# Cross attention of a decoder layer on one core: units spread one to a head, offsets and keys in halves, two transposed buffers, positions in 12 operations, clips ahead of unit copies

## The reference

```python
K = k @ Wk.T + bk; V = v @ Wv.T + bv; Qp = q @ Wq.T + bq
off = (Qp @ Woff.T + boff)                  # 16 heads x 5 samples
loc_x = mod(ref + off + loc, sign_lens)
ix = ((loc_x / (key_len - 1) * 2 - 1 + 1) * key_len - 1) / 2
x0 = floor(ix); dx = ix - x0; i0 = x0; i1 = i0 + 1
sk = 0.5 * ((1 - dx) * gather0(Kh, i0) + dx * gather0(Kh, i1))
sv = 0.5 * ((1 - dx) * gather0(Vh, i0) + dx * gather0(Vh, i1))
attn = softmax(einsum(Qh / sqrt(16), sk)); ctx = einsum(attn, sv)
x = layernorm(x + ctx @ Wo.T + bo)
```

## Time and profile before

| | us |
|---|---|
| median of 3 runs | 2228.5 (2226.14 to 2231.98) |
| the profiled execution, its own time | 2223.39 |
| its span in the profile | 2221.6 |
| VectorE's first product of cross attention starts at | 1444.7 |
| VectorE's last product of cross attention starts at | 2021.7 |

### The profile page before, as it was taken

The page is one execution under the profiler, slowest core; times in us unless marked ns, Lnnn a source line. Parts: engine busy times, 40 slices in busy tenths (PEclk is TensorE's granted clock), DMA queues, the critical chain, the costliest instruction groups (busy, mean ns, idle before and its releaser), DMA issues. The chain is left out here.

```text
span 2221.6 us, 42277 instructions
## 1 busy us (share of the span) xinstructions
PE 1860.2 (84%) x16907; PEld 1111.1 (50%) x16907; DVE 1673.1 (75%) x2216; ACT 1311.9 (59%) x1718; POOL 1416.4 (64%) x1067
## 2 busy tenths in 40 slices
PE   5989999999999999999999996487887787883575
PEld 2535545545545545545545543365665565663332
DVE  4876876887887887887797761669769768778676
ACT  2556566656565566566565561286856756873476
POOL 2577877876966976976876873334654554555347
PEclk8989999999999999999999998799988898997796
DMA  6122212202213203213203200100000000100002
GB/s 198 43 48 67 63 44 68 71 16 68 71 35 75 65 15 77 64 33 77 63 16 77 51 23 25 55 3 7 2 7 2 2 2 2 44 2 1 2 1 76
DMA packets 57507, 92.33 MB, mean 42 GB/s; under 512 B 25312, under 2 KB 35552, under 8 KB 53344
## 3 DMA queue, kind: packets, MB, share of 16 engines
q1 hardware_dynamic: 48096, 89.36, 15.6%
q10 hardware_dynamic: 9216, 0.27, 0.2%
HBM read 51.33 MB, written 4.46 MB: 25 GB/s over the span
## 5 line engine op out<-in xcount | busy, mean ns | idle before, releaser
L930 POOL TENSOR_TENSOR acc<-acc,probs 128x1024 f32<-128x1024 f32 (+3 forms) x320 | 593.8, 1856 | 54.3 <-ACT probs L643 24.8
L587 ACT ACTIVATE chunks<-psum 128x1024 bf16<-128x1024 f32 x288 | 281.9, 1026 | 157.6 <-PE psum L453 116.8
L643 ACT ACTIVATE probs<-psum 128x1024 f32<-128x1024 f32 (+3 forms) x384 | 290.7, 812 | 114.8 <-PE psum L494 114.8
L486 PE MATMUL psum<-operands 64*128 64x512 f32 (+3 forms) x1536 | 310.2, 512 | 24.8 <-ACT chunks L587 18.1
L1488 ACT ACTIVATE onehot<-psum 128x1024 bf16<-128x1024 f32 x320 | 323.0, 1038 | 1.3 <-PE psum L1298 1.3
L1895 POOL TENSOR_TENSOR vs<-vs,wgt 128x1280 f32<-128x1280 f32 x64 | 156.3, 2442 | 245.1 <-DVE wgt L1739 245.1
L1316 PE MATMUL psum<-pieces,onehot 128*128 128x64 bf16 x7680 | 289.0, 199 | 25.3 <-ACT vs L1495 18.7
L1316 PEld LDWEIGHTS psum<-pieces,onehot 128*128 128x128 bf16 x7680 | 260.6, 102 | 88.6 <-issue 46.0
L510 PE MATMUL psum<-probs,vals 128*64 128x512 f32 (+3 forms) x1536 | 292.2, 501 | 13.4 <-POOL probs L909 8.3
L786 DVE TENSOR_REDUCE lows<-chunks 128x2 f32<-128x1024 bf16 (+1 forms) x224 | 266.6, 1214 | 22.1 <-ACT chunks L587 12.2
L909 POOL TENSOR_SCALAR_AFFINE_SELECT probs<-probs 128x256 f32<-128x256 f32 x256 | 153.9, 619 | 103.0 <-ACT probs L643 103.0
(11 more groups left out here) (228 smaller groups left out, 3431.4 us busy)
## 6 DMA issues: line engine op xcount, KB each, us to landing
operands<-turned SPq DMA_DIRECT2D x124, 256.0 KB, 5.1
rden<-inverse_rows SPq DMA_DIRECT2D x64, 256.0 KB, 3.9
raw<-in_wqk SPq DMA_DIRECT2D x30, 256.0 KB, 4.4
y<-in_x SPq DMA_DIRECT2D x1, 4096.0 KB, 16.4
wo<-in_wo SPq DMA_DIRECT2D x16, 256.0 KB, 2.7
out<-res SPq DMA_DIRECT2D x16, 256.0 KB, 2.1
raw<-in_wv SPq DMA_DIRECT2D x15, 256.0 KB, 4.3
raw<-in_xT SPq DMA_DIRECT2D x12, 256.0 KB, 3.7
```

What stands on the lines that cost most here:

```text
L486: nc.tensor.matmul(dst[:, hh, 0:width], ops[n % OBUF][rows, 1, kt * P:(kt + 1) * P].bitcast(F32), ops[n % OBUF][rows, 0, a:a + width].bitc ...
L587: nc.scalar.activation(chunks[k % MBUF][:, :, :], slot("max", n, c)[:, :, :], ACT.Copy, scale=-1.0)\
L643: nc.scalar.activation(probs[u % PBUF][:, :, 0:width], slot("s", n, u)[:, :, 0:width], ACT.Exp, scale=1.0 / D ** 0.5).then_inc(s_exp, 1)
L930: G.tensor_tensor(dst, dst, src, ALU.add).then_inc(s_acc, 1)
```

## The change

It changes the following, all in cross attention; everything else is as it was.

- At most one unit stands in a head, at its step 0 (`i0` stays at head 14, step 3): inputs' transposes at heads 0 and 1, offsets in two halves at 2 and 3, `cT` at 4 and 5, keys and values in two halves at 6 and 7, `out` at 8 and 9, queries at 10 and 11.
- `tT` becomes two buffers, `x1T` and `outT`, so that the input's transposes of the next batch can stand while the output's of the batch before are made; the waits on `s_wo` and `s_qd` change with it.
- `locate` has 12 parts with one instruction each, at heads 4, 5, 8, 9, 12 and 13. A table of positions (`ref + loc + folded bias`) is made once and added when the offsets are read.
- ScalarE issues the clips of a step ahead of the unit's copy, for every unit.
- The last batch's input is normalised in the first batch (heads 0 and 3), no longer in the third; statistics of the batch before move to heads 10 and 11, its normalisation to heads 13 and 14, `lengths` to head 3.
- GpSimd's queue follows: `bias_x1` ahead of round 0, `split_kv` ahead of round 1, then `x2_deviations`, `bias_q`, round 2.

```diff
-EARLIER_AT = {(4, 0): ("cT", 0), (4, 2): ("cT", 1), (5, 0): ("out", 0), (5, 2): ("out", 1)}
+EARLIER_AT = {(4, 0): ("cT", 0), (5, 0): ("cT", 1), (8, 0): ("out", 0), (9, 0): ("out", 1)}
-LATER_AT = {(6, 0): ("x1T", 0), (6, 2): ("x1T", 1), (7, 1): ("kv", 0), (8, 1): ("off", 0),
...
+LATER_AT = {(0, 0): ("x1T", 0), (1, 0): ("x1T", 1), (2, 0): ("off", 0), (3, 0): ("off", 1), (6, 0): ("kv", 0),
+            (7, 0): ("kv", 1), (10, 0): ("q", 0), (11, 0): ("q", 1), (14, 3): ("i0", 0)}
-LOCATE_AT = [(9, 2), (9, 3), (10, 1), (10, 3), (11, 1), (11, 3), (12, 1), (12, 3), (13, 1), (13, 3)]
+LOCATE_AT = [(4, 1), (4, 3), (5, 0), (5, 1), (5, 3), (8, 1), (8, 3), (9, 1), (9, 3), (12, 1), (12, 3), (13, 1)]
+X1_STATISTICS_AT = [(0, 1), (0, 2)]
+X1_NORMALISE_AT = [(3, 0), (3, 1), (3, 2), (3, 3)]
+X2_STATISTICS_AT = [(10, 1), (11, 1)]
+X2_NORMALISE_AT = [(13, 2), (13, 3), (14, 0), (14, 1)]
...
-        tT = sb("tT", [P, KT, S])
+        x1T, outT = (sb(name, [P, KT, S]) for name in ("x1T", "outT"))
+        table = sb("positions", [P, TT, HK])
...
                 for u in range(UNITS):
                     use = unit_at(b, h, u)
-                    if use and use[0] == "i0" and n + 1 < HEADS_ALL:
+                    if n + 1 < HEADS_ALL:
                         for k in AHEAD[u]:
                             make_onehot(n + 1, k)
+                    if use:
                         copy_unit(*use)
-                    else:
-                        if use:
-                            copy_unit(*use)
-                        if n + 1 < HEADS_ALL:
-                            for k in AHEAD[u]:
-                                make_onehot(n + 1, k)
                     copy_values(n, u)
...
+            def set_table():
+                st.then(V.tensor_tensor(table[:, :, :], over(ref.unsqueeze(1), [P, TT, HK]),
+                                        over(loc.unsqueeze(2), [P, TT, HK]), ALU.add))
+                dve.wait_ge(s_fold, 1)
+                V.tensor_tensor(bfold[:, :], slot("fold", 0, 0)[:, 1, 0:HK], boff, ALU.add).then_inc(s_foldb, 1)
+                dve.wait_ge(s_foldb, 1)
+                V.tensor_tensor(table[:, :, :], table[:, :, :], over(bfold[:, :].unsqueeze(1), [P, TT, HK]), ALU.add)\
+                 .then_inc(s_table, 1)
...
-                    st.then(V.tensor_scalar(c, a, inv, MAGIC, ALU.mult, ALU.add))
+                    st.done(V.tensor_scalar(c, a, inv, MAGIC, ALU.mult, ALU.add))
+                elif part == 1:
                     st.done(V.tensor_scalar(d, c, MAGIC, size, ALU.subtract, ALU.mult))
...
+                elif part == 7:
+                    dve.wait_ge(s_i0t, b)
+                    st.done(V.tensor_scalar(row, in_pairs(d), MAGIC, None, ALU.subtract))
                 elif part == 8:
-                    dve.wait_ge(s_i0t, b)
-                    for n, src in enumerate((e, d)):
-                        st.done(V.tensor_copy(i0b[:, :, :, HP * NK * n:HP * NK * (n + 1)],
-                                              src.rearrange("p t (g n) -> p t g n", g=NHP)))
+                    st.done(V.scalar_tensor_tensor(out=in_pairs(a), in0=in_pairs(c), scalar=-0.5, in1=row,
+                                                   op0=ALU.add, op1=ALU.subtract))
```

More of the change, by code:

```diff
@@ L1329, in transpose_x1, with project_kv @@
                 last.then_inc(s_x1T, 1)
-            def project_kv(b):
+            def project_kv(b, v):
                 pe.wait_ge(s_in, 32 * (b + 1))
[L1333 to L1338, removed]
+                wait_slot("kv", b, v)
+                dst = slot("kv", b, v)
+                for kt in range(KT):
+                    last = nc.tensor.matmul(dst[:, 0, :], ctxT[:, v, kt, :], wkv[:, kt, :],
+                                            start=kt == 0, stop=kt == KT - 1)
                 last.then_inc(s_kv, 1)
@@ L1643, in read_off @@
-            def read_off(b):
-                dve.wait_ge(s_off, b + 1)
-                src = slot("off", b, 0)
-                for hf in range(2):
-                    ins = V.tensor_tensor(dx[b % 2][:, 4 * hf:4 * hf + 4, :],
-                                          src[:, hf, 0:4 * HK].rearrange("p (t n) -> p t n", n=HK),
-                                          over(bfold[:, :].unsqueeze(1), [P, 4, HK]), ALU.add)
-                    if hf:
-                        ins.then_inc(s_offr, 1)
+                st.settle()
@@ new lines, in scale_kv @@
+                V.tensor_tensor(kvt[:, :, :], slot("kv", b, v)[:, 0, :].rearrange("p (s e) -> p s e", s=2), kvb, ALU.add)\
+                 .then_inc(s_kvr, 1)
+                dve.wait_ge(s_kvr, 2 * b + v + 1)
+                for s in range(2):
+                    ins = V.tensor_scalar(kvd[:, :, 2 * s + v, :], kvt[:, s, :].rearrange("p (h d) -> p h d", d=HD),
+                                          valid[:, v:v + 1], 0.5 if s else 0.5 * HD ** -0.5, ALU.mult, ALU.mult)
+                    if v and s:
+                        ins.then_inc(s_kvd, 1)
@@ L1655, in locate, with read_off @@
+            def read_off(b, hf):
+                dve.wait_ge(s_off, 2 * b + hf + 1)
+                tiles = slice(4 * hf, 4 * hf + 4)
+                V.tensor_tensor(dx[b % 2][:, tiles, :], slot("off", b, hf)[:, 0, 0:4 * HK].rearrange("p (t n) -> p t n", n=HK),
+                                table[:, tiles, :], ALU.add).then_inc(s_offr, 1)
             def locate(b, part):
@@ L1659, in locate, with in_pairs @@
                 c, d, e = (o[:, :, :] for o in off)
+                def in_pairs(x):
+                    return x.rearrange("p t (g n) -> p t g n", g=NHP)
+                row, square_high, square_low = (i0b[:, :, :, HP * NK * n:HP * NK * (n + 1)] for n in range(3))
                 st.settle()
                 if part == 0:
-                    dve.wait_ge(s_offr, b + 1)
+                    dve.wait_ge(s_offr, 2 * (b + 1))
                     dve.wait_ge(s_len, b + 1)
-                    st.then(V.tensor_tensor(c, a, over(ref.unsqueeze(1), [P, TT, HK]), ALU.add))
@@ L1788, in _ @@
             dve.wait_ge(s_const, 16 * 4)
-            dve.wait_ge(s_fold, 1)
-            V.tensor_tensor(bfold[:, :], slot("fold", 0, 0)[:, 1, 0:HK], boff, ALU.add).then_inc(s_foldb, 1)
-            dve.wait_ge(s_foldb, 1)
-            read_off(0)
+            set_table()
+            for hf in range(2):
+                read_off(0, hf)
             for part in range(len(LOCATE_AT)):
-                if part == len(LOCATE_AT) // 2:
-                    scale_kv(0)
+                if part in (5, 7):
+                    scale_kv(0, (5, 7).index(part))
                 locate(0, part)
```

141 lines of the change are left out of this document (65 added, 76 removed).

## The result

The changed kernel took **2235.2 us** (median of 14 runs) beside 2225.8 for the kernel before in the same session: a ratio of **1.0039, interval 1.0024 to 1.0054**, 9.4 us slower. The forecast was 2181.5. Two of the 14 runs (2327.9 and 8878.7 us) and one of those beside them (2312.2) were slow and are left out of the ratio. The profiled execution's own time is 2232.8 us, its span 2230.8.

A forecast was written before the change was run, and what follows sets the result against it. It took a ring of three engines over two PSUM slots as the bound. Savings of 15.7 + 16.0 + 7.2 + 1 (batches) + 7 (ahead of the first head) = 47 us gave 2181.5 us, range 2150 to 2213.

The forecast's parts named there:

- What bounds the kernel: Cross attention: three engines go round in a ring over two PSUM slots; one long insertion makes the two others wait.
- Base and units: Second batch: 107.6 us for four plain rounds, plus 26.3 us for the units spread over its heads.
- 2.75 and 2.4 us: Cost today of each `cT` unit in head 4 and each `out` unit in head 5, as read from the profile.
- 12 + 2.8 + 2.9 + 2.7 = 20.4 us: Second batch, VectorE's extra work: `locate`, statistics, normalisation, then lengths with aggregation; charged as 10.7 us of batch time.
- the forecast's 0.4 and 0.79: Batch time per us of extra VectorE work: 0.79 in heads without a long unit, 0.4 mostly beside units.
- the forecast's 0.36: Cost of each us that TensorE stands at 1.2 GHz, read from head 15: 8.2 us against 10.6.
- I cost the order at nothing: GpSimd's reordered queue: same work, `split_kv` with all of head 8 to finish in, so no cost.
- Ahead of the first head: Before cross attention's first head: seven fewer `locate` instructions save 8.5 us, some 1.5 us is added; 7 less, between 2 and 9.
- VectorE meets GpSimd: Rival: five positions and the normalisation are stretched where values are weighed, 8.3 us a batch; 26 less, 2202 us; chance 0.14.
- TensorE falls to half rate: Rival, the slower outcome: 130 us more at half rate cancels the saving; 2260 to 2338 us; chance 0.04.
- The ring hides more: Rival: units cost only TensorE's excess, VectorE's extras vanish; middle batches near 130 us, 92 less, 2136 us; chance 0.17.
- The signs named in advance: Profile signs of a wrong forecast: heads 13, 14 above 11 us, positions over 2 us in heads 5, 9, clock below 0.85.

The follow-up runs named there:

- a_light: The changed kernel with GpSimd's weighing of values cut to a tenth of its multiplications and sums: 2167.6 us, ratio 0.9721.
- a_normonly: The changed kernel with only the normalisation moved to head 12, GpSimd's bias of the queries left where the change put it: 2210.7 us, ratio 0.9939.
- a_norm12: The changed kernel with the normalisation at head 12 and `bias_q` back behind round 2's weighing: 2201.5 us, ratio 0.9873.
- best_q12: a_best with the two units of the queries at heads 12 and 13 instead of 10 and 11: 2165.1 us, ratio 0.9712.
- b_twelve: The kernel before with only the table and twelve position instructions, at its own heads 9 to 13: 2194.2 us, ratio 0.9848.
- a_best: a_norm12 with positions only at heads 3, 4, 7, 8, 11 and 12, and keys and values scaled straight from PSUM: 2176.8 us, ratio 0.9785.

## Why the prediction was wrong

- **What bounds the kernel** was read rightly: a ring of three engines with two PSUM slots, in which something long ahead of a product is paid by all.
- **Base and units: about right, in part by luck.** With little weighing the batches are 132.3 and 144.0 us for the 132.1 and 144.6 forecast, and 148.4 and 116.6 for 144.6 and 115.8; but in the second the positions are 4.2 us below the sum's 12 and the softmax's first sum 5.0 above its undisturbed 1.3. The reading behind the prices was off: "The two `cT` units make head 4 last 11.9 us" and "The two `out` units make head 5 last 10.6" put each step 0 unit into its own head. Head 4 held a `cT` and an `out`, head 5 an `out` and an `x1T`, so 2.75 and 2.4 us are means of mixed pairs, and head 9, read as VectorE's positions alone, held a `q` unit. Heads 11 to 13 alone give the same 0.8 a us (7.5 us for 9.4).
- **VectorE: the step that failed**, "that makes 12 + 2.8 + 2.9 + 2.7 = 20.4 us". It took durations from the places where the instructions stood and charged them in the new ones. In the second batch `locate` is 15.3 us for 12, the normalisation 10.6 for 2.9, and two items are missing from the sum: the keys' scaling, which moved from a place without weighing into head 5 (3.1 us more), and the softmax's first sum (4.2 more, 3.5 of it at the end of head 11). That is 3.3 + 7.7 + 3.1 + 4.2 = 18.3 us of VectorE more than the sum had, and the batch is 22.1 us longer than forecast. The others miss by 11.1, 19.1 and 9.2 us: 61.5 in all, less the 5.1 gained ahead of the first head. In the second batch the delays cost 1.2 us each for the forecast's 0.4 and 0.79. Whether those rates were too low is open, because the half rate is in it: by the granted clocks 0.87 and 0.96, twice the missing part times the length is 43.3 us at 1.2 GHz for 11.5 in `a_light`. At the forecast's 0.36 the difference is 11 us, less where TensorE waited anyway; without these 11 us the delays would cost 0.6 a us.
- **"I cost the order at nothing"**, of GpSimd's queue, asked only whether each GpSimd result comes in time. It does. What was not asked is which VectorE instruction the moved `bias_q` runs beside; that cost 9 to 15 us (`a_normonly` against `a_norm12`).
- **Ahead of the first head:** 12.1 us for 7 (2 to 9). The term that was off was `locate`: 27.67 us became 11.95, 15.7 less, where 10.2 was the upper end; the 3.6 us between 15.7 and 12.1 stand against the 1.5 charged for the table and the second half of the offsets. The upper end priced each dropped instruction at the old mean of 1.46, and the twelve that stayed fell to 1.00 too.
- **The rivals.** "VectorE meets GpSimd" was the mechanism, with a chance of 0.14 and a price of 8.3 us a batch; the batch missed by 22. Its 10.5 us for positions and normalisation met 11.0 by luck: it had 7.5 and 3, the runs 3.3 and 7.7. It did not list the keys' scaling and the softmax's sum (7.3 us together), and it stretched each position by 1.5 us, read off one row (0.54 to 2.55 us), when what an instruction loses is whatever is left of GpSimd's, up to 4.5 us. "TensorE falls to half rate", the only case given for slower, had 0.50 in head 14 for it, and over the four batches the time at 1.2 GHz rose from 93 to 124 us, by twice the missing part of each batch's clock: at 0.36 that is 11 of the 21.6 us that the batches grew. No run parts it from VectorE's delays, which came with it and left with it; it was far from the 130 us more that this rival asked for. "The ring hides more" was half true once the collisions were gone: `best_q12` is 59 us below before, of the 92 that it priced. Its 130 us a batch scale TensorE's 114.7 by ScalarE's ratio, 26.9 over 23.8; with TensorE's own, 26.9 over 22.0, they are 140, and the middle batches of `best_q12` are 140.2 and 139.3.
- **The signs named in advance were useful:** heads 13 and 14 above 11 us and a position of over 2 us in head 5 (2.63) both came. The third, a clock below 0.85 in a middle batch, did not (0.87 and 0.89).
- **Left open:** halving the offsets and keys, and the second transposed buffer, were not tried alone; nor was the half rate apart from its causes; and the keys in PSUM are worth 13.6 us beside moved positions, while on top of `a_norm12` no gain is shown.

## What to carry to other kernels

When work on VectorE is spread over a loop, lay each moved instruction, and each VectorE instruction beside a moved GpSimd one, against GpSimd's timeline; a free slot of VectorE is no free slot if GpSimd is in a long instruction there. If it can't be moved, let it take one input from PSUM. And where a change moves much and gains little, cut the suspected neighbour's work to a tenth in both kernels: two runs showed here that the weighing cost the changed kernel 40 us more than the kernel before, and that the rest of the change was sound. And when heads are measured from product to product, look up in the timeline which units fall into a stretch before pricing them.

## What the runs showed of the hardware

- A VectorE instruction of 0.33 us took 3.78 us and ended 0.2 us behind a 4.50 us one of GpSimd; a pair of 0.8 us took 5.81 beside one of 4.54. The delay is the rest of GpSimd's instruction, not a share of a bandwidth. The Trainium skill ("SBUF — State Buffer", section "SBUF: two separate sides") states an exclusive lock on the port pair that VectorE and GpSimd share, held for a whole instruction; these rows agree with it.
- Not every VectorE instruction takes part. The products, which read PSUM, kept to 0.47 to 0.49 us in the midst of weighing, reductions too (0.47 us), and two scalings that read PSUM and SBUF kept to 480 ns where the same work from SBUF alone took 1107 ns on average.
- It works both ways: in head 5 GpSimd's sums took 1.55 us at the end and 2.01 at the start, where VectorE's positions stand. This one began while L1678 was running:

```profile
1617.77 2.01 POOL L1905 TENSOR_TENSOR vs<-vs 128x640 f32<-128x640 f32 x1
```

- Twelve instructions took 15.28 us in the places of the change, 11.45 in those of `b_twelve` and 7.65 in those of `a_best`: the same program text, by where it stands.
